# A graph network and MLP layer on one core: plain gathers, masks on ScalarE, reordered chunks, and the softmax matrix among the last products

## The reference

```python
xn = layernorm(x)
feat = concat([xn[src], xn[dst]], 1)                      # 8192 x 2048
e_f  = relu(feat @ W_kind + b_kind)                       # hh: 256 edges, oo: 1280, ho: the rest
logit = e_f @ W_a + b_a
m  = segment_max(logit, dst); ex = exp(logit - m[dst])
alpha = ex / segment_sum(ex, dst)[dst]
z  = segment_sum(alpha[:, None] * xn[src], dst)           # 512 x 1024
gnn = relu(concat([xn, z], 1) @ (W_hn for nodes 0..127, W_on for the others) + b)
q, k, v = split(xn @ w_qkv + b_qkv)                       # 16 heads of 64
mix = (elu(q) + 1) @ ((elu(k) + 1)^T v), divided by (elu(q) + 1) . sum(elu(k) + 1), @ w_proj + b_proj
x  = x + gnn + mix
out = x + bit_linear_mlp(layernorm(x))                    # 1024 -> 128 -> 1024, quantised, gelu, layer norm
```

## Time and profile before

| | |
|---|---|
| median of 3 runs | 779.29 us |
| profiled execution | 781.34 us, its span 779.6 us |
| TensorE matmul busy | 638.6 us (82%) |
| VectorE busy | 535.8 us (69%) |
| ScalarE busy | 229.2 us (29%) |
| GpSimd busy | 225.2 us (29%) |
| mean granted TensorE clock | 0.909 |
| DMA traffic | 167.54 MB, mean 215 GB/s |

### The profile page before, as it was taken

The page is one execution under the profiler, slowest core; times in us unless marked ns, Lnnn a source line. Parts: engine busy times, 40 slices in busy tenths (PEclk is TensorE's granted clock), DMA queues, the critical chain, the costliest instruction groups (busy, mean ns, idle before and its releaser), DMA issues.

```text
span 779.6 us, 8283 instructions
## 1 busy us (share of the span) xinstructions
PE 638.6 (82%) x2687; PEld 469.5 (60%) x2689; DVE 535.8 (69%) x1128; ACT 229.2 (29%) x294; POOL 225.2 (29%) x175
## 2 busy tenths in 40 slices
PE   4999999999789588995996995995655676898952
PEld 3888888888668476883884653784540111686621
DVE  7878633666778794675766789334679886327996
ACT  3343243233332154434223551431230100311001
POOL 3000324665546553653764510000000000002340
PEclk9999999999979889997997998999687699799985
DMA  9654749999999997999998953561721230140202
GB/s 344 239 189 161 244 137 335 367 362 361 365 364 367 346 309 215 314 280 292 275 343 281 277 174 90 202 228 69 282 96 55 63 153 1 60 135 5 108 28 81
DMA packets 43963, 167.54 MB, mean 215 GB/s; under 512 B 5392, under 2 KB 5776, under 8 KB 36752
## 3 DMA queue, kind: packets, MB, share of 16 engines
q1 hardware_dynamic: 20736, 88.81, 31.0%
q0 software_dynamic: 20160, 73.41, 30.3%
q10 hardware_dynamic: 3024, 4.79, 2.4%
HBM read 150.21 MB, written 16.78 MB: 214 GB/s over the span
## 4 chain that ended last, share of the span: by engine, by line
PE 31%; DVE 26%; DMA 18%; issue 13%; ACT 5%; POOL 5%; DVEq 1%; ACTq 0%; POOLq 0%
DMA gathered_rows<-edge_tables,dst_row 15%; PE bank_low L1462 7%; PE bank_low L1463 7%; PE bank_low L1464 7%; DVE gathered_rows L1075 3%; POOL gathered_rows L583 3%; DMA w_raw<-in_wt 3%; DVE w_lo L893 2%; DVE hot_src L1276 2%; ACT w_hi L658 2%; PE bank_high L1657 2%; DVE gathered_rows L1069 2%; POOL gathered_dst L583 1%; DVE running_max L1099 1%; PE bank_high L1658 1%
## 5 line engine op out<-in xcount | busy, mean ns | idle before, releaser
L1462 PE MATMUL bank_low<-w_hi,xT_hi 128*128 128x512 f32 x484 | 196.4, 406 | 42.6 <-ACT bank_low L686 27.5
L1463 PE MATMUL bank_low<-w_lo,xT_hi 128*128 128x512 f32 x484 | 193.8, 400 | 0.0
L1464 PE MATMUL bank_low<-w_hi,xT_lo 128*128 128x512 f32 x484 | 193.2, 399 | 0.0
L658 ACT ACTIVATE w_hi<-w_raw 128x2048 fp32r<-128x2048 f32 x49 | 93.7, 1915 | 166.5 <-DMA w_raw<-in_wt 85.4
L1075 DVE SCALAR_TENSOR_TENSOR gathered_rows<-gathered_rows,wa_bc 128x1024 f32<-128x1024 f32 x68 | 83.4, 1227 | 75.4 <-DMA gathered_rows<-edge_tables,dst_row 73.0
L1462 PEld LDWEIGHTS bank_low<-w_hi,xT_hi 128*128 128x128 f32 x484 | 94.3, 195 | 66.4 <-ACT bank_low L686 23.9
L893 DVE TENSOR_TENSOR w_lo<-w_raw,w_hi 128x2048 fp32r<-128x2048 f32 x48 | 109.5, 2287 | 30.8 <-ACT w_hi L658 30.6
L1464 PEld LDWEIGHTS bank_low<-w_hi,xT_lo 128*128 128x128 f32 x484 | 94.2, 195 | 20.5
L1463 PEld LDWEIGHTS bank_low<-w_lo,xT_hi 128*128 128x128 f32 x484 | 94.5, 195 | 19.4
L583 POOL DMA_INDIRECT gathered_rows<-edge_tables,src_row x68 | 94.2, 1385 | 40.4 <-DMA edge_tables<-stage 20.0
L618 POOL TENSOR_TENSOR small<-small,nhalf 128x1 f32<-128x1 f32 x12 | 10.7, 891 | 258.5 <-DVE small L1356 245.6
(11 more groups left out here) (271 smaller groups left out, 945.8 us busy)
## 6 DMA issues: line engine op xcount, KB each, us to landing
w_raw<-in_wt SPq DMA_DIRECT2D x54, 1024.0 KB
edge_tables<-stage SPq DMA_DIRECT2D x32, 256.0 KB
bias_bc<-in_bias_rows ACTq DMA_DIRECT2D x16, 256.0 KB
x_in<-in_x SPq DMA_DIRECT2D x4, 512.0 KB, 9.1
xn_scratch<-xn SPq DMA_DIRECT2D x4, 512.0 KB, 5.9
node_top<-stage SPq DMA_DIRECT2D x8, 256.0 KB
x_part<-in_x SPq DMA_DIRECT2D x8, 256.0 KB, 6.0
mix_out<-stage SPq DMA_DIRECT2D x8, 256.0 KB
```

The lines of the kernel that those rows point to most:

```text
L658: act.activation(w_half(c, h)[0], raw[:, h, :], ACT.Copy).then_inc(w_hi_done, 1)
L1462: pe.matmul(dest, lh, rh, start=start and i == 0, stop=False, skip_group_check=True)
L1463: pe.matmul(dest, lh, rl, start=False, stop=False, skip_group_check=True)
L1464: last = pe.matmul(dest, ll, rh, start=False, stop=last_one, skip_group_check=True)
```

## The change

- `ADDED_HERE` is now every tile: each tile is two plain gathers, and VectorE adds them all. `SLOTS` is 5 and `SECOND` is 5.
- The masks come from ScalarE as |FAR x (node - dst)|, FAR = 2^110, into eight buffers (`MASKS`), queued ahead of the chunk's copies. The running maximum is a running minimum of mask - logit.
- The chunks' order is T0, T1, T2, T3, T4, HHT0, T5, HHB0, T6, HHT1, T7, HHB1, and then as before. The head-edge chunks have banks 4 to 7 of their own, opened by four products with zeros; their bias seeds come after that. Their masks have a buffer of their own.
- `TILES` is spread anew, up to PR1 instead of ON0. The additions of x to PR0 and PR1 move behind the tiles of the next chunk.
- The destinations by tile are transposed by TensorE (after K0's first row of the second half), stored to DRAM, and broadcast back in three DMAs from GpSimd after the last tile, over the row buffers.
- The maxima: TensorE transposes the running minima in the middle of PR1, VectorE reduces them and splits them into three bf16 parts; after PR1 a one-hot matrix of four tiles at a time (one VectorE instruction, two buffers) is multiplied by the parts, 3 columns per tile, which gives the maximum of each edge. GpSimd's reduction goes.
- The softmax matrix: VectorE makes the destination one-hot for four tiles in one instruction and the source one-hot per tile (four buffers); ScalarE scales the former with the exponent's halves (eight buffers each). TensorE makes tiles 0 to 23 between ON1's row blocks, the others after it.
- A is transposed unscaled; 1/den is applied where the bottom product is added to the top. The halves of xn, BON0 and BON1 are made in another order: xn's and BON0's after the last scaled one-hot, BON1's high halves between the copy of A and its transposed copy, its low halves among z's products.

```diff
-TILES = {4: (0, 1), 5: (2, 3), 6: (2, 3), 7: (2, 3), HHT0: (2, 1), HHB0: (1, 1), HHT1: (2, 1), HHB1: (1, 2),
-         K0: (3, 2), V0: (3, 2), K1: (4, 2), V1: (3, 2), Q0: (4, 2), Q1: (4, 2), HN0: (2, 0), ON0: (4, 2)}
+TILES = {HHT0: (1, 1), T5: (1, 3), HHB0: (3, 1), T6: (1, 3), HHT1: (3, 1), T7: (0, 3), HHB1: (3, 1), K0: (0, 3),
+         V0: (2, 2), K1: (3, 4), V1: (2, 3), Q0: (3, 4), Q1: (2, 3), HN0: (1, 1), ON0: (0, 1), PR0: (2, 3),
+         PR1: (2, 2)}
 assert sum(map(sum, TILES.values())) == T_GATHERED
-LAST_EDGES = ON0
-MAXIMA = {PR1: (0, 24), ON1: (24, 56)}
-T_EARLY = 56
-SLOTS = 8
+LAST_EDGES = PR1
+SLOTS = 5
 LAG = 2
-SECOND = 2
+SECOND = 5
...
-ADDED_HERE = [t for t in range(T_GATHERED) if t % 2]
+ADDED_HERE = list(range(T_GATHERED))
...
+MAX_AT, LOOKUP_AT = (PR1, 0, 3), (PR1, 1, 3)
+A_AT = {(ON1, 0, 1): (0, 3), (ON1, 0, 2): (3, 8), (ON1, 1, 0): (8, 13), (ON1, 1, 1): (13, 18), (ON1, 1, 2): (18, 24)}
+A_LATER = 24
+HOT_BEFORE = {(ON1, 0): (0, 8), (ON1, 1): (8, 13), (ON1, 2): (13, 18)}
+MASKS = 8
+HOT = 8
+GROUP = 4
...
+            if c in HH:
+                bank_of[c, i] = (4 if c in (HHT0, HHB0) else 6) + i
...
+        pool.wait_ge(dst_stored, 16)
+        pool.wait_ge(edge_dot, T_GATHERED)
+        flat = dst_d.rearrange("t e -> (t e)")
+        for i, (a, b) in enumerate(((0, 24), (24, 48), (48, UT))):
+            pool.dma_start(dst_bc[:, a * P:b * P], flat[a * P:b * P].partition_broadcast(P)).then_inc(dst_loaded[i], 16)
...
+        def copy_dst():
+            act.wait_ge(dst_psum, 1)
+            act.activation(dst_t[0:UT, :], bank[6][0:UT, 0:P], ACT.Copy).then_inc(dst_copied, 1)
+            act.wait_ge(dst_copied, 1)
+            act.dma_start(dst_d, dst_t[0:UT, :]).then_inc(dst_stored, 16)
+        masked = [0]
+        def masks(c, h):
+            for t in range(masked[0], masked[0] + TILES.get(c, (0, 0))[h]):
+                if t == 0:
+                    act.wait_ge(idx_ready, 7)
+                if t >= MASKS:
+                    act.wait_ge(edge_max, t + 1 - MASKS)
+                act.activation(other[:, t % MASKS, :], one_up, ACT.Abs, scale=FAR, bias=far_dst[:, t:t + 1]).then_inc(edge_mask, 1)
+                masked[0] = t + 1
...
+        def hot_tiles(first, end):
+            for t in range(first, end):
+                if t < T_GATHERED:
+                    at, s, w = hot_dst[:, t // GROUP % 2, t % GROUP * P:(t % GROUP + 1) * P], t % HOT, 1
+                    if t % GROUP == 0:
+                        act.wait_ge(hot_dst_done, t // GROUP + 1)
+                    if t >= HOT:
+                        act.wait_ge(hot_used, t + 1 - HOT)
...
+                hi, lo = (x[:, s:s + w, :].rearrange("p w n -> p (w n)") for x in (hot_hi, hot_lo))
+                act.activation(hi, at, ACT.Copy, scale=ex_hi[:, t:t + 1]).then_inc(hot_done, 1)
+                act.activation(lo, at, ACT.Copy, scale=ex_lo[:, t:t + 1]).then_inc(hot_done, 1)
...
+        hot_tiles(A_AT[ON1, 1, 2][0], UT)
+        act.wait_ge(xnr_loaded, 16 * MT)
+        act.wait_ge(hot_T_used, T_GATHERED // GROUP + 2)
+        for k in range(KT):
+            act.activation(xn_hi[k][:, :, :], xn_raw[:, :, k * P:(k + 1) * P], ACT.Copy).then_inc(xn_hi_done, 1)
+        hi_half(BON0, 0)
         hi_half(BON0, 1)
...
+            dve.wait_ge(edge_mask, t + 1)
+            dve.wait_ge(edge_dot, t + 1)
+            dve.scalar_tensor_tensor(out=best, in0=other[:, t % MASKS, :], scalar=logit[:, t:t + 1], in1=best,
+                                     op0=ALU.subtract, op1=ALU.min).then_inc(edge_max, 1)
...
+        def reduce_maxima():
+            dve.wait_ge(run_psum, 1)
+            step(dve.tensor_reduce(least[:, :], bank[4][:, :].rearrange("p (b n) -> p b n", n=P), AX.X, ALU.min))
...
+            dve.tensor_copy(parts[:, :, 2], rest[:, :]).then_inc(parts_ready, 1)
+        def look_up():
+            dve.wait_ge(places_ready, 2)
+            groups = T_GATHERED // GROUP
+            for g in range(groups + 2):
+                if g * GROUP in (0, 24, 48):
+                    dve.wait_ge(dst_loaded[g * GROUP // 24], 16)
+                if g >= 2:
+                    dve.wait_ge(hot_T_used, g - 1)
+                if g < groups:
+                    dve.tensor_scalar(hot_T[:, g % 2, :], dst_bc[:, g * N:(g + 1) * N], place_of[:, 0:1], None, ALU.is_equal).then_inc(hot_T_done, 1)
...
+            dve.wait_ge(hot_T_used, groups + 2)
+            dve.tensor_reduce(mx_e[:, :], bank[5][:, 0:3 * UT].rearrange("p (t i) -> p t i", i=3), AX.X, ALU.add).then_inc(mx_read, 1)
+            dve.wait_ge(mx_read, 1)
...
+        def hot_group(g):
+            first = g * GROUP
+            if g >= 2:
+                dve.wait_ge(hot_done, 2 * GROUP * (g - 1))
+            dve.tensor_tensor(hot_dst[:, g % 2, :].rearrange("p (t n) -> p t n", n=P), along(one_up, GROUP, P),
+                              spread(dst_f[:, first:first + GROUP], GROUP, P), ALU.is_equal).then_inc(hot_dst_done, 1)
+            for t in range(first, first + GROUP):
+                hot_source(t)
+        def hot_source(t):
+            if t >= 4:
+                dve.wait_ge(hot_used, t - 3)
+            dve.tensor_scalar(hot_src[:, t % 4, :], iota[:, :], src_f[:, t:t + 1], None, ALU.is_equal).then_inc(hot_src_done, 1)
...
+            if c == HN0:
+                invert_den(0)
+                for j in range(4):
+                    add_kq("q", 1, j)
...
+            if c in (PR1, HN1):
+                for i in range(MT):
+                    add_x(PR0 if c == PR1 else PR1, i)
+            if c != ON1:
...
+            if c == PR1:
                 catch_up()
+                reduce_maxima()
+                lo_half(HN1, 1)
+                look_up()
+                exponents()
...
+        for g in range(1, T_GATHERED // GROUP):
+            hot_group(g)
+        hot_hh()
+        for k in range(KT):
+            dve.wait_ge(xn_hi_done, k + 1)
+            dve.tensor_tensor(xn_lo[k][:, :, :], xn_raw[:, :, k * P:(k + 1) * P], f32(xn_hi[k][:, :, :]), ALU.subtract).then_inc(xn_lo_done, 1)
+        lo_half(BON0, 0)
...
-                dve.tensor_tensor(top[:, m, cols], bank[q % 3][:, :], top[:, m, cols], ALU.add).then_inc(bot_evac, 1)
+                dve.scalar_tensor_tensor(out=top[:, m, cols], in0=bank[q % 3][:, :], scalar=rden[:, m:m + 1], in1=top[:, m, cols],
+                                         op0=ALU.mult, op1=ALU.add).then_inc(bot_evac, 1)
...
+        def transpose_maxima():
+            pe.wait_ge(edge_max, T_GATHERED)
+            pe.wait_ge(hh_max, 2)
+            pe.wait_ge(tmp_used, use_of("z", 1, 3) + 1)
+            pe.wait_ge(zb_copied, KT)
+            for b in range(NB):
+                ins = pe.transpose(bank[4][:, b * P:(b + 1) * P], run[:, b * P:(b + 1) * P], ident[:, :])
+            ins.then_inc(run_psum, 1)
...
+        def look_up():
+            words = load_blocks()
+            pe.wait_ge(parts_ready, 1)
+            groups = T_GATHERED // GROUP
+            for g in range(groups):
+                pe.wait_ge(hot_T_done, g + 1)
+                for t in range(g * GROUP, (g + 1) * GROUP):
+                    at = hot_T[:, g % 2, t % GROUP * P:(t % GROUP + 1) * P]
+                    last = pe.matmul(bank[5][:, 3 * t:3 * t + 3], at, parts[:, bass.ds(block_of(words, t), 1), :].rearrange("p b i -> p (b i)"),
+                                     start=True, stop=True, skip_group_check=True)
+                last.then_inc(hot_T_used, 1)
...
+        matrix_words = []
+        def matrix_tiles(first, end):
+            if first == 0:
+                pe.wait_ge(mx_read, 1)
+                for b in range(NB):
+                    pe.matmul(bank[4 + b][:, :], zeros[:, :], iota[:, :], start=True, stop=True)
+                matrix_words.extend(load_blocks())
+            for t in range(first, end):
+                pe.wait_ge(hot_src_done, t + 1)
+                pe.wait_ge(hot_done, 2 * (t + 1))
+                if t < T_GATHERED:
+                    out = bank_high[:, bass.ds(block_of(matrix_words, t), 1), :].rearrange("p b n -> p (b n)")
+                    pe.matmul(out, hot_hi[:, t % HOT, :], hot_src[:, t % 4, :], start=False, stop=True, skip_group_check=True)
+                    pe.matmul(out, hot_lo[:, t % HOT, :], hot_src[:, t % 4, :], start=False, stop=True, skip_group_check=True).then_inc(hot_used, 1)
...
```

447 lines of the change are left out of this document (220 added, 227 removed).

## The result

The changed kernel takes 756.0 us (median of 4 runs, 752.9 to 756.4) against 780.8 us for the kernel before beside it: ratio 0.969, 95% interval 0.965 to 0.974. It is faster, by a third of what was forecast (706, range 675 to 742), and lies above the range. A later series gave 753.7 us (6 runs, ratio 0.965, 0.962 to 0.968); experiments are compared with that one.

What follows compares the result with a forecast made beforehand. Four stages before the tail were taken to have different limits, with TensorE bounding the edge stages again after the change, by 9%. Gains 11 + 42 + 24 - 4 = 73 us gave 706 us against the median 779.3, range 675 to 742.

Steps and rivals of the forecast that it cites:

- Head-edge chunks between the tables: 109.5 to 258.4 us: mixing fast and slow weight consumers, with own banks for head-edge chunks, leaves 4 of 15 us; gain 11.
- K0 to ON0: Stretch of 231.7 us falls to 190, with 12 of 54 us of gaps and low clock left; gain 42.
- PR0 to z: From PR0's start to the z product, 179.4 us falls to 155 with some low clock; gain 24.
- I take 12: Look-up of the maxima after PR1, nothing beside it on TensorE: 12 us, bounds 6 and 30.
- in ScalarE's queue ahead of the copy of the matrix: After the last scaled copies at 131: halves of x (4.3) and BON0's high halves (3.6) come first, z at 151, 155 with low clock.
- Tail: After z, 110.1 us: BHN0's load, the tops and the mix follow BON1's low half, late by about 4 us, bounds 0 to 8.
- (2): Late chain: TensorE idles while ScalarE scales (0.9 us a copy), look-up takes 20 us, gain 24 goes to 0: 730 us; chance 0.14.
- (1): Edge stages: VectorE or GpSimd is the pace, half of the gaps stay, total gain 45: 734 us; chance 0.20.

Runs made afterwards that it cites:

- e1: Changed kernel with ScalarE issuing the bias seeds ahead of the high half of the next chunk's second weight half, not behind it: 736.7 us, ratio 0.942.
- e9: e1 with the four head-edge chunks behind the tables T5, T6 and T7 again and the edge tiles spread for that order: 739.6 us, ratio 0.947.
- e0: The changed kernel unchanged, run again as reference: 753.7 us, ratio 0.965 to the kernel before.
- e4: Changed kernel with BON0's and BON1's weight halves behind the copies and splits of the softmax matrix, and BHN0's loads behind mix_out's rows: 741.7 us, ratio 0.950.
- e6: Changed kernel with the late chain reordered (HN1 before the look-up) and look-up products taking all four blocks at a fixed address: 731.6 us, ratio 0.937.
- e2: Changed kernel whose look-up products take block 0 at a fixed address and load no block words into registers: 738.3 us, ratio 0.945.
- e8: Changed kernel with e1, e4 and e6 together, plus VectorE's exponential sums in V0, V1 and Q1 ahead of that half's edge tiles: 703.4 us, ratio 0.901.
- e3: Changed kernel with every second tile's second row added by the gather again, with 8 and 2 buffers as before: 770.4 us, ratio 0.986.
- e5: Changed kernel with the 68 masks made on VectorE again, straight ahead of the running minimum that reads them: 773.2 us, ratio 0.990.
- e11: Changed kernel with the masks made on VectorE, each ahead of its tile's dot product: 754.2 us, ratio 0.965.

## Why the prediction was wrong

The forecast was 73 us of gain in four terms (11, 42, 24, less 4). Measured by the traces it was 25 of span: less 6.9 up to K0, 35.2, less 2.3 and less 1.0. Two terms failed outright.

- **Head-edge chunks between the tables: gain 11, got a loss of 6.9.** The failed step is "get banks of their own, so seeds of K0 no longer wait for the head-edge reads". The banks were free, and K0's late wait for the head-edge reads (9.73 us at 275.41) is indeed gone, but the seeds came late all the same, since ScalarE issues them behind a high half whose load SyncE issues behind a table's stores. The prediction checked the banks and not the queue. By the lengths of the chunks (this is argued, no run tells it apart): before, such a wait had a table chunk of 21.8 us to hide in, now it has a head-edge chunk of 10.9. e1 alone moves K0 to 247.2, where the prediction had put it (247). So the bound of the stretch was right, the wait was missed. The mixture of the chunks itself matters little: e9 has it at 0 to 4 us of time.
- **K0 to ON0: gain 42, got 35.2.** Right in kind and nearly in size (190 forecast, 196.5 measured; of the gaps left, that at HN0 is 5.12 us where 2 to 4 were put, and e1 leaves it). Experiments tell three causes apart, each by one trace: plain gathers 13.8 us of the stretch, tiles moved out 19.4 for nine of them (some 15 for the seven that the change moved, if each counts alike), masks at most 7.5 and by the medians nothing. The prediction gave the gathers the leading part and counted of the tiles only those of HN0 and ON0 (14 us of VectorE). The 19.4 us are in part a loan: PR0 to z pays 7.1 back, in the waits for PR1's seeds and for the last minimum. The latter was forecast at 4 and is 4.74 in the first trace, but 1.72 in e0, where the former is 3.87 instead of 1.87: the two together are 6.6 and 5.6.
- **PR0 to z: gain 24, got a loss of 2.3.** The failed step is the look-up, "I take 12": 516.9 to 538.5 is 21.6 us, since each product's address is worked out in registers. Next to it the order behind the look-up: HN1's seeds wait for PR1's additions, which VectorE does behind look-up and exponents (gap 3.86), and ON1's seeds stand behind a high half that waits for a load behind PR1's stores (4.29), the same kind as at T6. ON1 starts 93.1 us behind PR0, forecast 72.5. From ON1's start to the last scaled copy it took 66.6 us where 58.5 had been put; a part of that is that a tile's two scaled copies take 0.585 us, not 0.54, for 50 tiles instead of 44, the rest stays open. The end, from the last scaled copy (621.5) to z, took 22 us and had been put at 24, "in ScalarE's queue ahead of the copy of the matrix": right, and e4 shows that 11 of it was only order. e4 gives 11.0 us and e6, which contains what e2 gives (10.8), 22.0; together in e8 the stretch is 145.0, below the 155 of the forecast.
- **Tail: loss 4, got 1.0.** BHN0's later load was covered: from z on TensorE has no gap of 1 us up to 692.

Of the rivals, (2), "the late chain stays serial", came nearest for the late part: its look-up of 20 us was the measured size and its gain of 0 is close to the loss of 2.3, but its copies at 0.9 us a tile were not seen (0.585), and it left the gains before PR0 whole; it said 730. (1) had half of the gaps stay for the pace of VectorE or GpSimd. Between K0 and PR0 the gaps of over 1 us fell from 38.8 us to 8.7, and those ahead of K0 had another reason. Its GpSimd half is refuted. The median gather instruction did grow, from 967 ns to 1673 ns for the source rows, and GpSimd still waited 159.6 us for buffers. The Trainium skill, "SBUF — State Buffer", section "SBUF: two separate sides", has the port that the two share. The trace agrees as far as the median goes (it is 964 ns in e3, with half of the additions), while the mean only went from 1385 to 1458 ns; the price lay beside other work.

The range failed because its upper end took both losses only in part. Each alone, 18 us less before K0 or 26 less behind PR0, would have ended inside it (706 + 18 = 724, 706 + 26 = 732); both, with 7 us missing between K0 and PR0 and 3 saved in the tail, are 754.

What stays open: in e5 K0 starts 13.2 us sooner than in e0, in e11 with the masks on VectorE as well only 2.3. The traces tell where, in the same three gaps at T6, T7 and K0: they hold 14.1 us in e0, 11.9 in e11 and 4.9 in e5. Why the seeds come so much sooner in e5 no run tells.

## What to carry to other kernels

When a change shortens a stage that hid something, read the in-order queue of every engine across it: an instruction that frees or fills a bank must not stand behind one that waits for a load for later work. The profile names only the last link of such a chain; the load behind the stores stood two queues away. Price an instruction whose address is worked out in registers by its pitch, from start to start, not by its duration.

## What the runs showed of the hardware

- TensorE products whose operand address is worked out in registers (a shift and a mask of a word for each) were 0.31 us apart (68 in 20.6 us), the same with a fixed address 0.09 us (68 in 5.9 us), though the durations are alike, 183 and 164 ns. In the softmax matrix, where two 128x512 products share such an address, a tile's pair took 0.43 us at its fastest, no more than two passes, and the price isn't seen. Twelve columns in place of three took 172 ns (e6); that look-up, with other work of VectorE in it, took 8.7 us, and picking afterwards 2.4 us of VectorE: still the cheaper way.
- A ScalarE copy of 128x128 from SBUF took 389 ns in the kernel after, one of the same size from PSUM 272 ns; the latter had been taken as the price of masks and scaled copies. Two in a row start 0.292 us apart. The two differ in more than the memory: the former also reads its scale, one value for each partition. The groups of the kernel after, shown below, tell the two apart: such values (`nbq`) make the same operation 89 ns longer, while without them a Gelu on SBUF (`y`) is 36 ns longer than a copy from PSUM (`z`), and at 128x512 a copy takes 613 ns from SBUF (`xn_hi`) and 599 from PSUM (`xT_hi`). The Trainium skill, "Perfetto Trace Analysis", section "Optimizing Scalar/DVE Operations", gives ScalarE a larger fixed cost on SBUF (about 93 ns) than on PSUM (about 51 ns), with about twice this in the profiled duration. The trace agrees in direction; 14 to 36 ns are less than half of the 84 that this would make.

```profile
L751 ACT ACTIVATE tmp<-bank_low,nbq 128x512 f32<-128x512 f32 x8 | 5.5, 687 | 22.6 <-DVE qT L1224 17.3 <-PE bank_low L1544 5.3
...
L751 ACT ACTIVATE tmp<-bank_low 128x512 f32<-128x512 f32 x8 | 4.8, 598 | 13.2 <-DVE kbuf L1224 11.9 <-PE bank_low L1544 1.2
...
L892 ACT ACTIVATE z<-bank_high 128x128 f32<-128x128 f32 x8 | 2.2, 272 | 0.0
...
L901 ACT ACTIVATE y<-y 128x128 f32<-128x128 f32 x4 | 1.2, 308 | 20.8 <-DVE y L1461 20.8
```

- VectorE's running minimum, whose address is worked out in registers too, waited 0.3 us for the mask made just before it (20.2 us in 68 in e5); with a dot product and mostly an addition between them it waited nothing that shows, and the whole kernel was 19 us faster. It is not the price of every operation that waits for the one before it: the splits of the maxima in the kernel after, each waiting for the last and at fixed addresses, start 0.04 us after it. That the registers are the reason is likely and not shown.

```profile
506.57 0.16 DVE L1258 TENSOR_TENSOR rest<-rest,parts 128x4 f32<-128x4 f32 x1
506.77 0.17 DVE L1259 CAST parts<-rest 128x4 bf16<-128x4 f32 x1
```
